# Mix stage in two halves of four groups, and the attention weights in two loads

## The reference

```
x = x + _L0_attn_ref(_L0_cond_ref(x, itok_B_1_198, L0_cond_weights), ln_g, ln_b, Wq, ...)

# _L0_cond_ref: one 32x32 matrix for each sequence, picked by an index
w = weights[conditions]
return jnp.einsum('bct,bcd->bdt', x, w)

# _L0_attn_ref: normalization over the 256 features, then the projections
mu = jnp.mean(X, axis=-1, keepdims=True)
var = jnp.mean(jnp.square(X - mu), axis=-1, keepdims=True)
Xn = (X - mu) * jax.lax.rsqrt(var + EPS) * ln_g + ln_b
Q = split_heads(Xn @ Wq + bq)
```

## Time and profile before

| what | us |
| --- | --- |
| three timed runs | 594.25, 598.15, 599.76 |
| their median | 598.15 |
| span of the profiled execution, first to last instruction | 583.4 |
| median less this span | 14.75 |
| TensorE busy in the span | 491.4 |

### The profile page before, as it was taken

The page is one execution under the profiler, slowest core; times in us unless marked ns, Lnnn a source line. Parts: engine busy times, 40 slices in busy tenths (PEclk is TensorE's granted clock), DMA queues, the critical chain, the costliest instruction groups (busy, mean ns, idle before and its releaser), DMA issues. The chain is left out here.

```text
span 583.4 us, 10868 instructions
## 1 busy us (share of the span) xinstructions
PE 491.4 (84%) x4205; PEld 372.0 (64%) x4205; DVE 360.4 (62%) x772; ACT 251.7 (43%) x545; POOL 261.7 (45%) x240
## 2 busy tenths in 40 slices
PE   2897799999998999998879899369989893089956
PEld 0586458886886788776653447257767582089956
DVE  3666568886687778854676464958777447034422
ACT  6167754443432444242872334366655241024430
POOL 5045435464353577774650000278870105526650
PEclk9889999999999999998999899859998976579987
DMA  5464763000000122230000008611100001398326
GB/s 171 168 238 141 318 193 90 1 1 1 0 1 1 37 63 64 64 85 35 2 3 1 1 1 321 220 39 27 25 19 2 2 0 62 102 353 284 123 67 206
DMA packets 24724, 51.51 MB, mean 88 GB/s; under 512 B 4265, under 2 KB 16706, under 8 KB 23521
## 3 DMA queue, kind: packets, MB, share of 16 engines
q1 hardware_dynamic: 18704, 40.60, 20.3%
q0 software_dynamic: 5968, 10.22, 5.8%
HBM read 43.97 MB, written 12.37 MB: 97 GB/s over the span
## 5 line engine op out<-in xcount | busy, mean ns | idle before, releaser
L754 PE MATMUL ps<-x_split,gate_up_split 128*128 128x512 f32 x384 | 96.4, 393 | 0.1
L754 PEld LDWEIGHTS ps<-x_split,gate_up_split 128*128 128x128 f32 x384 | 72.0, 188 | 17.2 <-issue 1.5
L2018 POOL DMA_INDIRECT wbig<-new_kv,prepi x40 | 42.9, 1073 | 80.2 <-DMA new_kv<-work 69.0
L947 POOL TENSOR_TENSOR gate_up_split<-wbig,gate_up_split 128x768 fp32r<-128x768 f32 (+1 forms) x24 | 41.6, 1734 | 52.4 <-ACT gate_up_split L887 52.3
L869 DVE TENSOR_TENSOR hidden_split<-work,hidden_split 128x512 fp32r<-128x512 f32 x34 | 37.8, 1110 | 23.1 <-ACT hidden_split L936 23.1
L936 ACT ACTIVATE hidden_split<-work 128x512 fp32r<-128x512 f32 x34 | 21.4, 630 | 59.6 <-DVE work L864 57.5
L778 PE MATMUL ps<-hidden_split,down_split 128*128 128x512 f32 x160 | 42.5, 395 | 2.6 <-issue 1.4
L1959 POOL DMA_INDIRECT chosen<-work,wbig x31 | 30.5, 984 | 28.9 <-issue 15.0
L953 POOL TENSOR_TENSOR down_split<-wbig,down_split 128x384 fp32r<-128x384 f32 (+1 forms) x24 | 29.1, 1213 | 25.9 <-ACT down_split L894 25.8
L2018 POOL DMA_INDIRECT wbig<-in_cache_dram,prepi x32 | 33.5, 1046 | 7.6 <-issue 7.1
L778 PEld LDWEIGHTS ps<-hidden_split,down_split 128*128 128x128 f32 x160 | 29.8, 188 | 10.7 <-issue 4.2
(11 more groups left out here) (326 smaller groups left out, 1174.8 us busy)
## 6 DMA issues: line engine op xcount, KB each, us to landing
work<-in_wE_dram SPq DMA_DIRECT2D x1, 5376.0 KB, 16.3
wbig<-in_wF_dram SPq DMA_DIRECT2D x3, 1664.0 KB, 6.9
sorted<-wmid SPq DMA_DIRECT2D x1, 3999.0 KB, 16.8
wbig<-in_wG_dram SPq DMA_DIRECT2D x1, 3072.0 KB, 10.4
wbig<-in_wE_dram SPq DMA_DIRECT2D x6, 384.0 KB, 3.8
wbig<-chosen SPq DMA_DIRECT2D x8, 256.0 KB, 4.7
wbig<-sorted SPq DMA_DIRECT2D x1, 1935.0 KB, 12.8
wmid<-in_wE_dram SPq DMA_DIRECT2D x5, 384.0 KB, 5.6
```

Of the source, the lines that this page charges most:

```text
L754: mm = nc.tensor.matmul(o, self.gus[:, w % 2, a, 2 * m + k, :], self.xs[:, b, k, n * HALF:(n + 1) * HALF], start=(k == 0 and a == b), stop ...
L947: nc.gpsimd.tensor_tensor(self.gus[:, k % 2, 1, 0:self.gu_chunks], self.gate_up[:, :, j * P:(j + 1) * P], self.gus[:, k % 2, 0, 0:self.gu_ ...
L2018: return nc.gpsimd.indirect_dma_start(dst, None, table, bass.IndirectOffsetOnAxis(ap=rows.bitcast(U32), axis=0), **({} if bound is None el ...
```

## The change

PE does four groups, then the transposes of these four, then the other four groups. DVE applies scale and shift to the first half ahead of the moments of the third pair. The attention's weights come in two loads: wq and wk after the second pair of gathers, as the whole was before, and wv and wo after the last pair, ahead of the rest of the small constants. value_rows(0) gets a wait for the second load.

```diff
@@ in Attention.tensor, behind scores(0), keys(1) and queries(1)
                 queries(1)
                 pe.wait_ge(sem(self.in_ready[0]), self.in_ready[1] + 4)
+                if self.biased:
+                    pe.wait_ge(sem("ld_wA_late"), 16)
                 value_rows(0)
@@ in SP's list
                 sp.wait_ge(sem(f"mix_gather{pair}"), 32)
                 if pair == 1:
-                    sp.dma_start(wmid[:, 0:2048], wA_d).then_inc(sem("ld_wA"), 16)
+                    sp.dma_start(wmid[:, 0:1024], wA_d[:, 0:1024]).then_inc(sem("ld_wA"), 16)
+            sp.dma_start(wmid[:, 1024:2048], wA_d[:, 1024:2048]).then_inc(sem("ld_wA_late"), 16)
             sp.dma_start(small[:, n_early:], small_d[:, n_early:]).then_inc(sem("ld_small"), 16)
@@ in DVE's list
             mix_normalize(0)
+            mix_affine(0)
             mix_moments(2)
-            mix_affine(0)
             mix_moments(3)
@@ in PE's list
-            for g in range(6):
+            for g in range(4):
                 mix(g)
             pe.wait_ge(sem("ld_early"), 16)
             mix_turn(0)
-            mix(6)
-            mix(7)
+            for g in range(4, NT):
+                mix(g)
             att_a.second_input = lambda: mix_turn(1)
```

## The result

The change made the kernel slower: 608.01 us against 598.95 us in the same set of runs (medians of six). The ratio on record, estimated from the single executions and not the quotient of the medians, is 1.0167 with a 95% interval of 1.0119 to 1.0215, so it is slower, and whether by more or less than 2% is open. The forecast was 598.0, the same as before.

The account below looks back on a forecast made before the run. TensorE was taken as the bound, busy 491.4 of 583.4 us; span 583.4 - 0.2 = 583.2, plus 14.75 around it, gave 597.95, rounded 598.0 us. The range was 593.4 to 601.5 us.

Parts of the forecast that it names:

- the new wait in value_rows(0): TensorE's wait at 33.57 us for the second load, landing at about 19: said to cost nothing.
- a rival on load traffic: In scores(0), x_feat's load overlaps a code fetch, which pays at most 2.7 us: 599.3 us, chance 0.05.
- The baseline: Profiled span of 583.4 us, with 14.75 us to the median taken as what lies around a span.
- The sum for the mix stage with the clock at its lower level: Transposes done at 16.66, third pair 18.55, fourth pair 19.62 us; keys(0) 0.2 us earlier than 19.84; chance 0.52.
- its bounds of 2.4 and 4.9: First 512 KB weight load lands between 2.4 and 4.9 us behind its issue, taken as 3.4, before keys(0).
- The second load and the constants behind it delay nobody: Second load adds 1.3 us; constants land at about 22.4 instead of 21.4, hidden from VectorE with 3 us to spare.
- a shift at the feed-forward carries to the end whole: A gain before keys(0) was said to reach the kernel's end whole, above nothing and below 0.2 or 1.5 us.
- The clock does not fall: Rival: clock holds at 15 us in the mix stage, -1.5 us, 596.65; 594.9 with second stretch spared; chance 0.22.
- Late clock: Rival: lower clock lasts until 22 us, over fourth pair, keys(0) and queries(0): +2.3 us, 600.45; chance 0.10.
- The rival on code: In scores(0), x_feat's load overlaps a code fetch: +1.15 us, 599.3; chance 0.05.
- slower by over 1%: Chance 0.03 that the whole kernel gets slower by more than about 1% (6 us).

Follow-up runs that it names:

- e8: Kernel before with only the new order of TensorE and VectorE, and the whole weight load issued behind the last pair of gathers: 584.35 us, ratio 0.9983.
- e12: e8 with TensorE's wait for the early constants taken out: 584.12 us, ratio 0.9992.
- e5: Kernel before with one more TensorE wait, at value_rows(0), for the first weight load, which had long landed: 589.01 us, ratio 1.0061.
- e4: Kernel before with only the weights in two loads and the wait for the second, old order: 607.99 us, ratio 1.0077.
- e9: Changed kernel, unedited, run again in the quick place: 586.74 us, ratio 1.0049 to before.
- e1: Kernel before, unedited, profiled once more: 603.82 us, one run.
- e3: Kernel before with only the new order of TensorE and VectorE, weights in one load: 606.52 us, ratio 1.0046.
- e14: e13 with both halves of the weights loaded behind the last pair of gathers: 603.42 us, ratio 0.9991 to before.
- e13: Changed kernel with its wait for the second load moved from value_rows(0) to ahead of the second transposes: 606.98 us, ratio 1.0029 to before.
- e2: Changed kernel, unedited, profiled once more: 609.54 us, ratio 1.0127 to before.
- e6: Changed kernel with both weight loads on one semaphore, waited for ahead of keys(0) and not again at value_rows(0): 585.97 us, ratio 1.0035 to before.
- e7: Kernel before with the whole weight load issued behind the last pair of gathers, old order: 586.47 us, ratio 1.0025.
- e11: Kernel before with one more idle TensorE wait, ahead of the second transposes: 585.13 us, ratio 0.9999.

## Why the prediction was wrong

**The step that failed** is the one on the new wait in value_rows(0): "it costs nothing, 14 us being there". That the load had landed was right, in every profile. I priced a wait by what it waits for, and forgot that it is an instruction in TensorE's list. At that place the fetch of the next code came late, in four profiles of five, which shows as a stop of 1.5 to 2.35 us inside scores(1) and, behind each of the four, as a stretch at 1.2 GHz over keys(2) and queries(2), 5.41 us or more instead of 3.7. (Such a stretch is not behind every stop: it follows ten of the 13 first ones, and not those of 1.91 us in the first profile after, 1.84 in e8 and 2.50 in e12.) Alone the wait costs 3.6 us (e5), enough for the changed kernel's whole loss of 2.7 us at the quick place. Of the 9 us between the medians of the result it is the part that is shown; the rest is open. Why a wait exactly there puts the fetch off is open. The row was in front of me: the stop of 2.01 us in the earlier trace rows and the packet beside it in the earlier trace rows. I used them only for a rival on load traffic, and asked there how the fetch might be slowed, not how its start might move.

The Trainium skill bears on this in Runtime: NRT & Kernel Launch, section Instruction fetch mechanics: code comes in blocks of 16 KiB, and the cost of crossing into the next is "one DMA tail-bump, mostly hidden". The trace agrees on the 16 KB. On the cost it does not: the first stop is there in both profiles of before, at 2.01 and 2.16 us, and the second, of 1.52 to 2.35 us, in e4, e5, e9 and the first profile after.

**The baseline.** The first profile stood for the quick kind of place and the timed runs for the slow kind. In the slow kind, all seven profiles have the second pair's count late: 13.54 us for the kernel before, 14.80 to 14.93 for the six others. The new order hangs everything on the first four groups' normalization, while the old order did the third pair meanwhile: keys(0) at 20.16 in e1 (19.84 in the first profile) against 23.12 and 22.12 in the two profiles of the changed kernel there. Part of this is that e1's count was less late; e4, with the old order and the count at 14.90, has keys(0) at 21.65, and e3, with the new order and the count at 14.93, at 22.54. So at an equally late count, these two place the new order about 1 us behind. It is tempting to call this the 0.46% of e3, but e14 has all of it and no loss (0.9991). What lies between the 1.27% and 1.67% of the changed kernel there and the 0.6% of the wait alone is open: moving the wait seems to give back about 1% (e13), and e2's one profile, of its quickest execution, has no stop to look at. What makes the count late is open; it is not the weight load (e14), and not the new order (e1, e4). I can't say either why it is less late in e1. Those seven traces also hold some 3,700 semaphore events where the other nine hold 4,850, so "remote" may only mean that the event which released VectorE was not recorded.

**What was right.** The sum for the mix stage with the clock at its lower level, in e9: transposes from 14.07 to 16.67 (16.66 in the sum), keys(0) 0.7 us earlier, where I had 0.2. The two late pairs took 2.54 and not 2.96 us; that the total came so near is partly luck, as e6, e8 and e12 need 3.16 to 3.57 for the same step. In e9 the two weight loads land in 4.2 us (median), within its bounds of 2.4 and 4.9, and the slowest gather in 3.9 instead of 5.0. The second load and the constants behind it delay nobody: the constants land in 7.4 us, and VectorE does not wait for them. x_feat still lands when the first code packet starts in e2, e7 and e9 (landing at 25.2, 26.8 and 25.4, packets at 24.56, 23.61 and 25.01), but the first two have no stop at all and e9's is 2.23 us, among the 1.84 to 2.55 of the others. Whether a shift at the feed-forward carries to the end whole can't be told from single executions, which differ by more behind that point: from the feed-forward's start to the end of the span it takes 507.15 us in the first profile of before and 504.13 in e9.

**The rivals.** "The clock does not fall" did not come about in e9, whose granted clock is 0.61 from 14.07 to 16.60 and 0.71 from there to 19.14. "Late clock" came about by half: in the first profile after and in e6, e8 and e12 the two late pairs took 3.22 to 3.64 us, so that by their length part or most of the fourth ran at the lower pace (the clock's records there start only about where these pairs end), but keys(0) and queries(0) took 3.72 to 3.94. The rival on code had the right object with the wrong mechanism. The bound for "slower by over 1%", 0.03, was too low because none of the cases contained a difference between places, although three runs of before at 594 to 600 beside a span of 583.4 called for one.

## What to carry to other kernels

Price a wait that never waits as an instruction: in a kernel whose trace shows "issue" stops in dense short matmuls, look up when the instruction queue's packets start, before and after the place where the instruction goes, and try new waits elsewhere (here ahead of the second transposes, at no cost). Before a sum is made on one profile, compare its span with the timed runs; 1.8 us lay around a span here, and anything more calls for a second profile. And a reordering that makes two engines hand work to and fro on an early result moves with that result: keys(0) started at 19.14 to 20.54 us where it was prompt and at 22.12 to 23.20 where it was late, against 19.84 to 21.65 in the old order. No gain from it shows in any timed run.

## What the runs showed of the hardware

- A wait for a load that had landed over 18 us before cost 3.6 us of 585 at one place in TensorE's list (e5), and another idle wait at another place cost nothing (e11).
- TensorE went on 2.2 to 2.7 us after the start of a code packet in all 17 stops of this kind.
- A TensorE matmul's count reached VectorE 0.06 to 0.08 us after the end of its record in the nine profiles of the quick place, and 1.6 to 3.2 us after it for one pair of groups in all seven profiles of the places where before takes 599 to 604 us.
- Those places also have a lower granted clock from 390 to 460 us: 0.72 to 0.84 in their seven profiles against 0.92 to 0.96 in the nine of the quick place, and 0.77 against 0.95 for the kernel before. In that stretch TensorE gets through 792 records in the first profile of before and 623 in e1; the two spans differ by 18.6 us.
